# Attention and ternary FFN on one core: first transfers in another order, gamma loads moved to SyncE's queue, and twelve unread products ahead of the first transposes

## What is computed

```python
x = x + xattn(ctx, layernorm(x), mask, ...)      # x: 1 x 2048 x 256, ctx: 1 x 1601 x 256
x = x + ffn(layernorm(x), w1, conv_w, conv_b, w2)

# xattn: 4 heads of 64
xn, ln = layernorm(ctx) * g + b, layernorm(latents) * g + b     # gains ln_x_g/b and ln_l_g/b
q = ln @ W_q
k, v = split(concat([xn @ W_kv, ln @ W_kv]))
sim = rmsnorm(q, q_gamma) * SCALE @ rmsnorm(k, k_gamma).T       # masked, softmax, @ v
return out @ W_out + b_out
# ffn: quantized x @ w1.T, depthwise conv of 3, silu, quantized @ w2.T
```

## Time and profile before

| | |
|---|---|
| median of 3 runs | 479.63 us (477.93 to 480.08) |
| the profiled execution, its own time | 480.25 us |
| its span in the trace | 478.2 us, so 2.05 us lie around the span |
| PE busy | 415.0 us (87%) |
| DVE busy | 391.1 us (82%) |
| ACT busy | 313.0 us (65%) |
| POOL busy | 78.3 us (16%) |
| mean granted TensorE clock | 0.968 of full |

### The profile page before, as it was taken

How to read it: one execution, slowest core, us unless ns; L and a number is a source line. 1 busy time by engine, 2 the same in 40 slices (tenths; PEclk the granted TensorE clock), 3 DMA queues, 4 the chain that set the end, 5 groups by cost and what they waited for, 6 DMA issues and landing times.

```text
span 478.2 us, 15103 instructions
## 1 busy us (share of the span) xinstructions
PE 415.0 (87%) x5910; PEld 282.9 (59%) x5910; DVE 391.1 (82%) x635; ACT 313.0 (65%) x359; POOL 78.3 (16%) x93
## 2 busy tenths in 40 slices
PE   0999985489999999999699899899899977798876
PEld 0666664146666666666476566666576644565664
DVE  4389999299978789879669878889878899999964
ACT  1356675156697766666556656656756567889866
POOL 2075554560000111010102002002001010000000
PEclk9999999599999999999999999999999995999989
DMA  8700000521211211111111111111111000010001
GB/s 231 183 1 1 1 2 10 179 94 45 67 46 35 68 35 45 58 35 45 48 36 45 56 36 45 58 34 45 41 33 42 1 0 2 0 45 23 24 24 66
DMA packets 27447, 22.56 MB, mean 47 GB/s; under 512 B 7229, under 2 KB 26878, under 8 KB 27390
## 3 DMA queue, kind: packets, MB, share of 16 engines
q1 hardware_dynamic: 25978, 21.72, 14.2%
q10 hardware_dynamic: 1412, 0.01, 0.2%
HBM read 7.04 MB, written 2.10 MB: 19 GB/s over the span
## 4 chain that ended last, share of the span: by engine, by line
PE 49%; DVE 21%; issue 14%; ACT 13%; ACTq 2%; DMA 1%; DVEq 1%
PE sc L1355 13%; DVE arena L698 7%; PE heads L1372 6%; PE heads L1373 5%; PE heads L1374 5%; ACT arena L1083 4%; PE heads L1251 3%; PE sc L1260 2%; PE by L1408 2%; ACT qq L1166 2%; ACT qq L1158 1%; DVE arena L592 1%; PE by L1528 1%; PE sc L1511 1%; PE heads L1511 1%
## 5 line engine op out<-in xcount | busy, mean ns | idle before, releaser
L698 DVE SCALAR_TENSOR_TENSOR arena<-arena 128x1024 bf16<-128x1024 f32 x160 | 196.2, 1260 | 40.3 <-ACT arena L1083 39.9
L1083 ACT ACTIVATE arena<-sc,kb 128x1024 f32<-128x1024 f32 x160 | 170.2, 1113 | 90.0 <-PE sc L1355 89.8
L1372 PEld LDWEIGHTS heads<-v,arena 128*128 128x128 bf16 x1280 | 117.7, 97 | 47.2 <-issue 34.2
L1372 PE MATMUL heads<-v,arena 128*128 (+1 forms) x1280 | 131.0, 194 | 10.3 <-DVE arena L698 8.9
L1355 PE MATMUL sc<-qs,kst 64*128 64x512 f16 x960 | 121.0, 385 | 11.7 <-issue 9.9
L1373 PE MATMUL heads<-v,arena 128*128 (+1 forms) x1280 | 129.6, 195 | 0.0
L1374 PE MATMUL heads<-v,arena 128*128 (+1 forms) x1280 | 129.0, 193 | 0.0
L1374 PEld LDWEIGHTS heads<-v,arena 128*128 128x128 bf16 x1280 | 119.1, 99 | 0.0
L1373 PEld LDWEIGHTS heads<-v,arena 128*128 128x128 bf16 x1280 | 118.9, 98 | 0.3
L1355 PEld LDWEIGHTS sc<-qs,kst 64*128 64x128 f16 x960 | 42.7, 95 | 59.2 <-issue 21.0
L470 POOL TENSOR_SCALAR frs<-fmv 128x2 f32<-128x2 f32 x8 | 7.0, 869 | 165.4 <-DVE fmv L750 165.4
(11 more groups left out here) (185 smaller groups left out, 590.5 us busy)
## 6 DMA issues: line engine op xcount, KB each, us to landing
kst<-kk SPq DMA_DIRECT2D x80, 128.0 KB, 2.0
xs<-in_x SPq DMA_DIRECT2D x8, 256.0 KB, 6.7
qs<-qq SPq DMA_DIRECT2D x16, 128.0 KB, 2.3
out<-cbuf SPq DMA_DIRECT2D x7, 256.0 KB, 2.1
xs<-in_ctx SPq DMA_DIRECT2D x6, 256.0 KB, 7.3
xs<-in_L_ffn_w SPq DMA_DIRECT2D x1, 1024.0 KB, 5.5
cbuf<-in_L_ffn_w SPq DMA_DIRECT2D x1, 1024.0 KB, 9.1
arena<-in_L_xattn_W_kv SPq DMA_DIRECT2D x1, 512.0 KB, 6.3
```

What stands on the lines that cost most here:

```text
L698: e.scalar_tensor_tensor(out=rest[:, j, :, :], in0=prob[:, j, :, :], scalar=SHRINK, in1=probh[:, j, :, :], op0=ALU.mult, op1=ALU.subtract) ...
L1083: a_.activation(prob[:, j, :, :], sc[j % 2][:, :, :], ACT.Exp, bias=kb[:, bass.ds(i * QUAD + j, 1)]).then_inc(exp_done[j], 1)
L1372: t_.matmul(o, hi, row[:, 0:OW], start=first and sub == 0, stop=False, skip_group_check=True)
```

## The change

Six edits:

- SP's first transfers were x pair 0, W_q, W_kv as one transfer, x pairs 1 to 7. They become x pair 0, the value half of W_kv (own semaphore `w_values`), x pair 1, the key half of W_kv, W_q, x pairs 2 to 7.
- The six gamma transfers leave ACT's queue and go on SP's, between the context and the masks.
- ACT's first `gains` waits for the four gains and biases alone (`ln_in`).
- PE no longer waits for the weights before its first transposes. The waits stand in front of the first values and the first queries and keys.
- `gamma_product` on DVE moves from turn -3 to turn -1.
- PE computes twelve 128x128 products of the identity and ones into a bank that nothing reads before it is written anew, ahead of the first transposes.

```diff
         def _(sp):
             sp.dma_start(xs[:, 0:2, :], xt[:, 0:2, :]).then_inc(d_x[0], 16)
+            sp.dma_start(wqkv[:, :, 2 * INNER:3 * INNER], w_kv[:, INNER:2 * INNER].rearrange("(k p) n -> p k n", p=P)).then_inc(s["w_values"], 16)
+            sp.dma_start(xs[:, 2:4, :], xt[:, 2:4, :]).then_inc(d_x[1], 16)
+            sp.dma_start(wqkv[:, :, INNER:2 * INNER], w_kv[:, 0:INNER].rearrange("(k p) n -> p k n", p=P)).then_inc(s["w_proj"], 16)
             sp.dma_start(wqkv[:, :, 0:INNER], w_q.rearrange("(k p) n -> p k n", p=P)).then_inc(s["w_proj"], 16)
-            sp.dma_start(wqkv[:, :, INNER:3 * INNER], w_kv.rearrange("(k p) n -> p k n", p=P)).then_inc(s["w_proj"], 16)
-            for n in range(1, XP):
+            for n in range(2, XP):
                 sp.dma_start(xs[:, 2 * n:2 * n + 2, :], xt[:, 2 * n:2 * n + 2, :]).then_inc(d_x[n], 16)
...
+            with nc.allow_non_contiguous_dma(reason="a few hundred numbers, one per partition"):
+                for i in range(2):
+                    sp.dma_start(gq[i * DH:(i + 1) * DH, 0:1], q_gamma.rearrange("(d a) -> d a", a=1)).then_inc(s["w_norm"], 16)
+                    sp.dma_start(gq[i * DH:(i + 1) * DH, 1:2], k_gamma.rearrange("(d a) -> d a", a=1)).then_inc(s["w_norm"], 16)
+            sp.dma_start(grow[64:65, 0:DH], q_gamma.rearrange("(a d) -> a d", a=1)).then_inc(s["w_norm"], 16)
+            sp.dma_start(grow[64:65, DH:2 * DH], k_gamma.rearrange("(a d) -> a d", a=1)).then_inc(s["w_norm"], 16)
             sp.wait_ge(s["zero_ready"], 1)
...
             def gamma_product():
-                dve.wait_ge(s["w_norm"], 16 * 10)
+                dve.wait_ge(s["w_norm"], 16 * 6)
...
-                if isinstance(i, int) and i == -3:
+                if isinstance(i, int) and i == -1:
                     gamma_product()
...
-                    act.dma_start(lng[:, i, :, 0], gain.rearrange("(k p) -> p k", p=P)).then_inc(s["w_norm"], 16)
-                    act.dma_start(lng[:, i, :, 1], bias.rearrange("(k p) -> p k", p=P)).then_inc(s["w_norm"], 16)
-                for i in range(2):
-                    act.dma_start(gq[i * DH:(i + 1) * DH, 0:1], q_gamma.rearrange("(d a) -> d a", a=1)).then_inc(s["w_norm"], 16)
-                    act.dma_start(gq[i * DH:(i + 1) * DH, 1:2], k_gamma.rearrange("(d a) -> d a", a=1)).then_inc(s["w_norm"], 16)
-            act.dma_start(grow[64:65, 0:DH], q_gamma.rearrange("(a d) -> a d", a=1)).then_inc(s["w_norm"], 16)
-            act.dma_start(grow[64:65, DH:2 * DH], k_gamma.rearrange("(a d) -> a d", a=1)).then_inc(s["w_norm"], 16)
+                    act.dma_start(lng[:, i, :, 0], gain.rearrange("(k p) -> p k", p=P)).then_inc(s["ln_in"], 16)
+                    act.dma_start(lng[:, i, :, 1], bias.rearrange("(k p) -> p k", p=P)).then_inc(s["ln_in"], 16)
             act.wait_ge(s["consts"], 1)
 
             a_.activation(largest_score[:, 0:1], halves[:, 0:1], ACT.Exp)
-            act.wait_ge(s["w_norm"], 16 * 10)
+            act.wait_ge(s["ln_in"], 16 * 4)
...
             pe.wait_ge(s["consts"], 6)
-            pe.wait_ge(s["w_proj"], 32)
+
+
+            for _ in range(12):
+                t_.matmul(bank[5][:, 0:P], ident[:, :], ones[:, :], start=True, stop=True)
...
                 wait(pe, "lnt_ready", n + 1)
+                if isinstance(n, int) and n == 0:
+                    pe.wait_ge(s["w_values"], 16)
...
             def project(n, kind, par):
+                if isinstance(n, int) and n == 0:
+                    pe.wait_ge(s["w_proj"], 32)
```

More of the change, by code:

```diff
@@ L219, in xattn_ffn @@
         probh = arena[:, 0:QUAD * 2 * CHUNK].bitcast(BF16).rearrange("p (k e c two) -> p k e c two", k=QUAD, e=2, two=2)[:, :, :, :, 1]
-        names = """w_norm w_rest w_proj mask_in w_ffn pairs_in ident_ready consts zero_ready count_step
+        names = """ln_in w_norm w_rest w_values w_proj mask_in w_ffn pairs_in ident_ready consts zero_ready count_step
             count_ready scale_ready limit_ready max_ps max_step max_taken qst_ready kq_ready shift_col shift_ps
```

## The result

The changed kernel takes 484.27 us in the median of 5 runs (482.95 to 485.72), against 479.63, also of 5. The recorded ratio is 1.0109, with a 95% interval from 1.0088 to 1.0129: slower by 1.1%. It isn't the quotient of the two medians, which is 1.0097. I had forecast 482.0 us, at most 484.0. The profiled execution took 485.72 us over a span of 483.8, and is the slowest of the five; the one of before had 480.25 over 478.2. So the spans differ by 5.6 us, one more than the medians, and the profile is read against these 5.6.

A forecast was written before the change was run, and what follows sets the result against it. PE carried half the last-ending chain; early on, DVE's pair 3 statistics, held by SP's list, were to bind. Terms -0.5 + 0.8 + 2.1 = +2.4 us raised the median from 479.63 to 482.0 us, range 479.2 to 484.0.

The forecast's parts named there:

- The early gain: At the start, ACT's gains and PE's first values were to come about 3.3 us earlier.
- the wait that I had named: DVE's statistics of pair 3 wait for SP's counting loop; of 3.3 us gained, 0.5 are left.
- `gamma_product` was hidden, as costed: On DVE behind pair 3, its 1.05 us costed at 0; at most 0.4 if PE weren't late.
- T3: Start of DVE's statistics of pair 3, 23.64 before; predicted 0.8 us later through SP's longer list, bounds 0 and 2.6.
- What I said would hide them: End of SP's list: 2.4 us of issuing `cb` and `bout` looked like queue waiting that could absorb the gammas' 2.1.
- -0.5: PE's values of pair 2 would start at 26.8 instead of 27.3 were the statistics of pair 3 unchanged.
- The clock, taken as 2.1: PE idles 3.6 us before the values of pair 2, then runs at half speed: loss 1.7 to 3.4.
- the long end of what I had named: After PE's idling, the half-speed stretch was to last 3.4 to 6.8 us; 6.8 is that end.
- I cost them at 0: The twelve products at PE's start run in idle time and end before the transposes, so cost 0; uncovered, 2.8 us.
- my +2.4: Whole-kernel sum of the predicted terms: 2.4 us slower, 0.5%, giving a median of 482.0 us.
- The products also ran longer than said: Twelve products on PE at the start were priced at 12 x 0.24 = 2.8 us, at the lower clock level.
- The rival that the products lift the clock: PE's pair 0 work at the upper clock, ready up to 3 us earlier, all taken back: 482.2 us; 10 in 100.

The follow-up runs named there:

- experiment 3: The changed kernel with DVE's statistics of pairs 3 to 7 waiting for their own transfers instead of SP's count of all pairs: 474.57 us, ratio 0.9909.
- experiment 5: The kernel before, with DVE's statistics of pairs 3 to 7 waiting for their own transfers: 478.83 us, ratio 1.0002.
- experiment 4: The changed kernel with twenty more unread products on PE in turn 0, ahead of the values of pair 2: 481.83 us, ratio 1.0051.
- experiment 2: The changed kernel with the six gamma transfers back on ACT's queue, behind the four gains: 482.95 us, ratio 1.0069.
- experiment 7: The kernel before with only the twelve unread products added, ahead of PE's wait for the weights: 481.17 us, ratio 1.0044.
- 11: The changed kernel with the old order of x and weights, W_kv as one transfer, gammas still on SP's list: 483.93 us, ratio 1.0082.
- 1: The changed kernel without its twelve products: 482.42 us, ratio 1.0054.
- experiment 6: The kernel before with six more small, unread transfers of the gammas' shape on SP's list, between context and masks: 480.12 us, ratio 1.0017.
- experiment 9: The changed kernel with pairs 3 to 7 waiting for their own transfers and without the twelve products: 476.27 us, ratio 0.9936.
- both of before: Two profiled executions of the unchanged kernel before: the first took 480.25 us, a later single repeat 478.18 us.
- 8: The changed kernel with pairs 3 to 7 waiting for their own transfers and 32 products of 48 columns replacing the twelve: 484.82 us, ratio 1.0122.
- 10: The changed kernel with pairs 3 to 7 waiting for their own transfers, plus 40 short half-precision products after the last projection: 475.28 us, ratio 0.9909.

## Why the prediction was wrong

**The mechanism at the start held; a cost elsewhere was missing.** The early gain was there in the predicted size: gains 8.91 (predicted 8.8), first values 9.98 (9.8), PE ready for the values of pair 2 at 23.1 (24.0). It was lost at the wait that I had named, the statistics of pair 3 behind SP's list; experiment 3, where the change without this wait is faster than the kernel before, shows that this wait decides, and experiment 5 that it didn't decide before. PE's idling brought the clock down; experiment 4 shows that this happens no more when PE is kept busy, and there the turn that took 8.65 us takes 5.60 again. `gamma_product` was hidden, as costed: DVE waited 2.43 us for ACT behind it.

**Two terms of the sum were too small, by 0.9 and 0.95 us.**
- *T3, taken as +0.8, measured +1.6.* I priced the six gammas at 0.35 us each by their nearest neighbours, the mask rows of a single piece. A transfer of 64 pieces took 0.59 to 1.09. Together they took 3.84, not 2.1. What I said would hide them, `cb` and `bout`, did hide 2.0 of it, and the mask rows 0.45. The start of the values of pair 2 is at +1.2, where the sum had -0.5 + 0.8 = +0.3.
- *The clock, taken as 2.1, measured 8.65 - 5.60 = 3.05.* The idling was 5.4 us, not 3.6, and the lower level lasted 6.8 us, the long end of what I had named. No row gave me that end, so it is luck that it fits.

**One term was missing:** +1.3 us for the stretch in attention in which PE waits for nothing that the profile shows, and 1.7 for the whole of attention. The stretch goes with the twelve products. In five executions with twelve products and nothing more the stretch is 4.5 to 5.0 (experiments 2, 3, 7, 11 and the change), in six without them 3.4 to 3.9 (1, 5, 6, 9 and both of before), and in three with yet more instructions 3.4 to 3.7 (4, 8, 10). That is shown. For the whole of attention there is one exception: 304.7 to 305.7 us in the five, 302.0 to 303.8 in five of the six, but 305.2 in experiment 9. That it is a matter of where the loop's instructions lie for PE's sequencer, as the expectations have it, is only argued. Experiment 7 gives the products' price alone, 1.0044.

**The step that failed** is "I cost them at 0", said of the products: I asked only whether they were covered where they stand, and they cost about 2 us by time (experiment 7) and 1.7 by the profile. It is the largest of the three errors, and with the other two it makes the 3.55 us between my +2.4 and the profile's 5.95.

The products also ran longer than said, 5.22 us instead of 2.8. I read the x8 behind 13.14 as eight products and halved the price for half the columns. The halving was right, 472 ns for 256 columns and 217 for 128. But each full-precision product is two instructions in the trace (x24 for twelve), so the x8 were four products and the price had to be doubled. They ended at 7.6, just ahead of the transposes at 7.89. The rival that the products lift the clock came true for a while. The four instructions of the first transposes took 0.63 to 0.66 us in all seven executions with the twelve products, and 1.09 in all six without. But only in experiments 3 and 11 was the clock still up in the first values (1.99 us); in the change they took 3.16, in the others up to 3.78 as before. What it brought was taken back at T3, as that rival said.

**The sum by the profile:** 1.2 + 3.05 + 1.7 = 5.95, against 5.6 between the spans; 0.3 of the first turns was made up before attention (96.27 - 92.33 = 3.94). The medians differ by 4.6, against a forecast of 2.4.

**How the shift of pair 3 splits** can be read from where SP gets to the first transfer behind the six of the context. From there to the start of pair 3 it took 11.9 to 12.1 us in the four executions without gammas on SP's list (both of before, 2 and 7), and 13.1 to 13.7 in the five with them (1, 4, 6, 11 and the change). So the gammas cost 1.0 to 1.9 net, 1.4 in the change. SP gets to that point at 11.2 to 11.7 with the old order and at 11.3 to 12.9 with the new one. The two overlap, and the change is at 11.8, so what the order costs stays open.

## What to carry to other kernels

Before a start is made faster, ask what holds the next stage: here one wait counted all transfers on a queue's own list, harmless until the engines in front were early enough to meet it. When small transfers are moved to another queue, price their issue by transfers of the same number of pieces, and look at what is queued behind them, if only a counter. And time a handful of added PE instructions in the whole kernel, since they can cost elsewhere than where they stand.

## What the runs showed of the hardware

- The length of an idle stretch of PE alone didn't tell whether the clock falls. It stayed up behind 2.60 us (experiment 2) and was at 0.50 behind 2.34 (experiment 6) and 2.08.
- A 128x48 product in full precision took as long as a 128x128 one at the lower level, 217 ns for each of its two instructions (13.86 us for 64, 5.22 for 24); from 256 columns to 128 the price had halved (3.78 us for 8).
- Issuing a transfer from SP's queue took 0.23 or 0.48 us for one row of 64 numbers, 0.59 to 1.09 for 64 pieces of 4 bytes, and 0.58 or 1.43 for 1024 pieces behind 1024 others. What makes the difference isn't shown.
- With twelve products (24 instructions) more at the program's start, one wait of PE some 230 us later was 4.5 to 5.0 us long in five executions, and 3.4 to 3.9 in six without them.
